# Graph attention on one core: transposes between projection chunks, denominators from three terms, batches written out

## The reference, cut to what matters

```python
h = jnp.maximum(_layernorm(x), 0.0)            # x: (8, 1024, 512)
q, k, v = heads(h @ Wq + bq), heads(h @ Wk + bk), heads(h @ Wv + bv)   # 16 heads of 32
scores = einsum('bhqd,bhkd->bhqk', q, k) / sqrt(32)
scores = where(adj[:, None] == 0, -inf, scores)
attn = softmax(scores, axis=-1)
out = einsum('bhqk,bhkd->bhqd', attn, v)       # heads side by side again: (8, 1024, 512)
return x + (out @ Wo + bo)
```

## Time and profile before

| | before |
|---|---|
| median of 3 runs (lowest to highest) | 2086.7 us (2085.78 to 2088.95) |
| the profiled execution: own time | 2085.51 us |
| the profiled execution: span of the trace | 2083.6 us |
| mean granted PE clock over the span | 0.989 |
| PE, DVE, ACT, POOL busy | 1932.5, 1557.3, 1478.1, 1302.1 us |
| chain that ended last | PE 76%, DVE 7%, issue 6%, DMA 5% |

### The profile page before, as it was taken

The page is one execution under the profiler, slowest core; times in us unless marked ns, Lnnn a source line. Parts: engine busy times, 40 slices in busy tenths (PEclk is TensorE's granted clock), DMA queues, the critical chain, the costliest instruction groups (busy, mean ns, idle before and its releaser), DMA issues.

```text
span 2083.6 us, 40441 instructions
## 1 busy us (share of the span) xinstructions
PE 1932.5 (93%) x14336; PEld 776.5 (37%) x14336; DVE 1557.3 (75%) x1587; ACT 1478.1 (71%) x1765; POOL 1302.1 (62%) x581
## 2 busy tenths in 40 slices
PE   3799899998999999999999999999899998999977
PEld 2334344343344333443334333334333343444312
DVE  5688777878768787687867877778767787767773
ACT  3577786677867788668876778767777677866672
POOL 0377567556666567656667557666557566676574
PEclk8999999999999999999999999999999999999999
DMA  5433244342444324343351434424234332442302
GB/s 177 122 87 96 82 112 132 88 107 64 120 112 124 83 76 132 86 122 86 92 142 56 115 93 117 119 74 119 81 109 122 88 106 66 117 122 64 74 1 81
DMA packets 103222, 206.61 MB, mean 99 GB/s; under 512 B 11616, under 2 KB 11744, under 8 KB 103008
## 3 DMA queue, kind: packets, MB, share of 16 engines
q1 hardware_dynamic: 103008, 203.80, 35.2%
HBM read 153.43 MB, written 50.33 MB: 98 GB/s over the span
## 4 chain that ended last, share of the span: by engine, by line
PE 76%; DVE 7%; issue 6%; DMA 5%; ACT 2%; POOL 1%; SPq 1%; DVEq 0%; ACTq 0%; POOLq 0%
PE ps L694 20%; PE ps L681 19%; PE ps L654 15%; PE ps L705 10%; PE ps L668 7%; PE ps L661 6%; DVE ring L905 4%; DMA k_stack<-k_parts 2%; DMA k_parts<-k_part 1%; SPq L513 1%; DMA edges<-adjT 1%; ACT hT_hi L776 1%; DVE k_part L918 1%; POOL acc L1079 1%; ACT ring L770 1%
## 5 line engine op out<-in xcount | busy, mean ns | idle before, releaser
L905 DVE TENSOR_TENSOR ring<-ps,mask 128x1024 f32<-128x1024 f32 x1024 | 1234.6, 1219 | 435.7 <-PE ps L681 399.9
L770 ACT ACTIVATE ring<-ring 128x1024 f32<-128x1024 f32 x1024 | 1069.7, 1051 | 382.9 <-DVE ring L905 374.6
L1079 POOL TENSOR_TENSOR acc<-ring 128x1024 f32<-128x1024 f32 x256 | 604.1, 2371 | 730.2 <-ACT ring L770 729.4
L681 PE MATMUL ps<-q_stack,k_stack 128*128 128x512 f16 x2048 | 610.4, 382 | 85.2 <-DVE ring L905 61.4
L1079 POOL TENSOR_TENSOR acc<-acc,ring 128x1024 f32<-128x1024 f32 x256 | 617.6, 2432 | 0.0
L694 PE MATMUL ps<-ring,v_sb 128*32 128x512 f32 x4096 | 509.1, 604 | 0.0
L681 PEld LDWEIGHTS ps<-q_stack,k_stack 128*128 128x128 f16 x2048 | 157.1, 98 | 481.8 <-DVE ring L905 246.4
L694 PEld LDWEIGHTS ps<-ring,v_sb 128*32 128x32 f32 x4096 | 100.9, 109 | 252.3 <-issue 218.1
L705 PE MATMUL ps<-acc,ones 128*32 128x512 f32 x1024 | 139.8, 597 | 2.7 <-issue 2.6
L705 PE MATMUL ps<-ring,ones 128*32 128x512 f32 x1024 | 137.3, 592 | 0.0
L661 PE MATMUL ps<-wv_hi,hT_hi 128*128 128x128 f16 x1024 | 103.1, 219 | 3.2 <-DVE k_part L918 3.2
(11 more groups left out here) (80 smaller groups left out, 1593.4 us busy)
## 6 DMA issues: line engine op xcount, KB each, us to landing
...
edges<-adjT SPq DMA_DIRECT2D x128, 256.0 KB, 2.9
q_stack<-q_parts SPq DMA_DIRECT2D x128, 256.0 KB, 4.9
k_stack<-k_parts SPq DMA_DIRECT2D x128, 256.0 KB, 5.0
...
```

Source lines behind the costliest of these rows:

```text
L681: i = nc.tensor.matmul(ps_s(j)[:, hh, :], stack["k"][:, up % 2, h, kt * P:(kt + 1) * P], stack["q"][:, up % 2, h, half * HALF:(half + 1) * ...
L770: nc.scalar.activation(tile, tile, ACT.Exp, scale=SCALE / UP / UP).then_inc(s["prob_ready"], 1)
L905: nc.vector.tensor_tensor(ring[:, slot_of(kt, pair), :].rearrange("p (a n) -> p a n", n=HALF), ps_s(j), mask[:, kt:kt + 1, half * HALF:(ha ...
L1079: nc.gpsimd.tensor_tensor(acc[:, group, pair, :], first_of, ring[:, slot_of(kt, pair), :], ALU.add).then_inc(s["sum_done"], 1)
```

## The change

Three things are changed together.

1. `BLOCKS` has four entries in place of five, the denominators have three terms in place of four (A, B and key tile 7): POOL adds key tiles 0 to 3 into A and 4 to 6 into B, ten additions a sweep in place of eight. The waits of POOL, DVE and PE on the sums follow.
2. The transposes have no slots of their own: they stand in `chunk_list` between the projection chunks of units 2 and 3, four in each, and the norms are in slot 29 of every unit. In unit 3 the second halves of q and k come behind all transposes. The slots in which x is normalised (by ACT) and loaded (by SP) follow.
3. The loops over batches 1 to 6 become Python loops on all engines: each batch is written out, with constants as semaphore targets.

```diff
-BLOCKS = {6: ("p0", "p1"), 10: ("p2", "p3", "dA"), 14: ("p4", "p5"), 16: ("p6", "dB", "d6"), 18: ("p7", "d7")}
-TERMS = "AB67"
+BLOCKS = {6: ("p0", "p1"), 10: ("p2", "p3"), 14: ("p4", "p5", "dA"), 18: ("p6", "dB", "p7", "d7")}
+TERMS = "AB7"
+SUMMED = {1: 0, 2: 2, 3: 4, 5: 6, 6: 8}
+SUMS = 10
+SUMMED_AT = {"A": 6, "B": 10}
...
-NORMALISE_AT = {(2, 5): 0, (2, 7): 1, (2, 9): 2, (2, 11): 3, (2, 23): 4, (2, 25): 5, (2, 27): 6, (2, 29): 7}
-T_AT = {(2, 19): 0, (2, 21): 1, (2, 23): 2, (2, 25): 3, (2, 27): 4, (2, 29): 5, (3, 1): 6, (3, 3): 7}
-SLOTS_OF = [SLOTS, SLOTS, [j for j in SLOTS if j <= 17], [j for j in SLOTS if j >= 5]]
-NORMS_AT = [29, 29, 18, 29]
+NORMALISE_AT = {(2, 5): 0, (2, 7): 1, (2, 9): 2, (2, 11): 3, (2, 21): 4, (2, 25): 5, (2, 29): 6, (3, 2): 7}
+NORMS_AT = 29
...
     if up == UNITS - 1:
-        return [] if last else ts + PROJ + [NORMS]
+        return [] if last else [q[0], ts[4], k[0], *ts[5:8], v[0], q[1], k[1], v[1], NORMS]
     if up == 2:
-        return PROJ + [NORMS] + ts
+        if last:
+            return [q[0], k[0], v[0], q[1], k[1], v[1], NORMS]
+        return [q[0], k[0], v[0], ts[0], q[1], ts[1], k[1], ts[2], v[1], ts[3], NORMS]
...
-            with pe.Fori(1, B - 1) as b:
+            for b in range(1, B - 1):
                 graph(b, False, False)
...
-                    pe.wait_ge(s["sum_done"], 8 * V + 4 * (TERMS.index(term) + 1))
+                    pe.wait_ge(s["sum_done"], SUMS * V + SUMMED_AT[term])
...
-                group, k = divmod(kt, 3)
+                group, n = kt // 4, SUMS * V + SUMMED[kt] + pair
                 pool.wait_ge(s["prob_ready"], U * TILES + j + 1)
...
-                        if j % SWEEP // PAIRS in (1, 2, 4, 5):
+                        if j % SWEEP // PAIRS in SUMMED:
                             sums(U, j, first and up == 0 and j < SWEEP)
```

More of the change, by code:

```diff
@@ L336, in chunk_plan @@
         return {}
-    plan = spread_out([c for c in chunks if c[0] != "t"], SLOTS_OF[up])
-    plan.update({at: [("t", t, 0, PIECES["t"])] for (u, at), t in T_AT.items() if u == up and ("t", t) in chunks})
-    return {**plan, NORMS_AT[up]: [(*NORMS, 0, PIECES["n"])]}
+    return {**spread_out(chunks, SLOTS), NORMS_AT: [(*NORMS, 0, PIECES["n"])]}
 def chunk_ends(up, first, last):
@@ L357, in count, with all_chunks, chunks_before, chunk_no @@
     return sum(c[0] in kinds for c in chunks)
[L360 to L374, removed]
-def two_before(b, up, first, chunk):
-    here = chunk_list(up, first, False)
-    i = here.index(chunk)
-    if i >= 2:
-        return b, up, first, here[i - 2]
-    if up:
-        return b, up - 1, first, chunk_list(up - 1, first, False)[i - 2]
-    if first:
-        return None
-    return b - 1, UNITS - 1, False, chunk_list(UNITS - 1, False, False)[i - 2]
+def all_chunks(b, up):
+    units = [(g, u) for g in range(b + 1) for u in range(UNITS) if (g, u) < (b, up)]
+    return [(g, u, c) for g, u in units for c in chunk_list(u, g == 0, g == B - 1)]
+def chunks_before(kinds, b, up):
+    return count(kinds, PRO_CHUNKS) + count(kinds, [c for _, _, c in all_chunks(b, up)])
+def chunk_no(kinds, b, up, chunk):
+    here = chunk_list(up, b == 0, b == B - 1)
+    return chunks_before(kinds, b, up) + count(kinds, here[:here.index(chunk)])
+def two_before(b, up, chunk):
+    here = chunk_list(up, b == 0, b == B - 1)
+    sequence = all_chunks(b, up) + [(b, up, c) for c in here[:here.index(chunk)]]
+    return sequence[-2] if len(sequence) >= 2 else None
 def fast_attention(nc, x, adjT, Wq, bq, Wk, bk, Wv, bv, Wo, bo, ident, headones, out, parts, flag):
@@ L438, in ps_s, with chunk_bank @@
             return ps[:, 2 * (j % 2):2 * (j % 2) + 2, :]
-        def chunk_bank(b, up, first, chunk):
-            n = chunk_no(ALL, 0 if first else 2, up, first, chunk) - len(PRO_CHUNKS)
+        def chunk_bank(b, up, chunk):
+            n = chunk_no(ALL, b, up, chunk) - len(PRO_CHUNKS)
             return ps[:, BANK_M + n % 2, :]
@@ L585, in graph @@
                             load_x(b + 1, (t + X_SLOTS) % QT)
-                        if (up, j - 1) in T_AT:
-                            t = T_AT[up, j - 1]
-                            sp.wait_ge(s["chunk_ready"], chunk_no(ALL, b, up, first, ("t", t)) + 1)
+                        for kind, t in ending_at(up, first, last, j - 1, "t"):
+                            sp.wait_ge(s["chunk_ready"], chunk_no(ALL, b, up, ("t", t)) + 1)
                             load_x(*((b + 1, t + X_SLOTS) if t + X_SLOTS < QT else (b, t + X_SLOTS - QT)))
@@ L599, in _ @@
             graph(0, True, False)
-            with sp.Fori(1, B - 1) as b:
+            for b in range(1, B - 1):
                 graph(b, False, False)
@@ L879, in _ @@
             graph(0, True, False)
-            with act.Fori(1, B - 1) as b:
+            for b in range(1, B - 1):
                 graph(b, False, False)
@@ L1040, in _ @@
             graph(0, True, False)
-            with dve.Fori(1, B - 1) as b:
+            for b in range(1, B - 1):
                 graph(b, False, False)
@@ L1104, in _ @@
             graph(0, True, False)
-            with pool.Fori(1, B - 1) as b:
+            for b in range(1, B - 1):
                 graph(b, False, False)
```

71 lines of the change are left out of this document (35 added, 36 removed).

## The result

| | before | after |
|---|---|---|
| median (lowest to highest) | 2087.8 us (2085.8 to 2091.1) | 2123.3 us (2118.9 to 2127.6) |
| the profiled execution: own time / span | 2085.5 / 2083.6 us | 2124.7 / 2122.9 us |
| ratio to before, 95% interval | | 1.0168 (1.0142 to 1.0195) |

The change makes the kernel 1.7% slower. The forecast was 2038.5 us, 85 us too low, and the measured time lies above the top of the range, 2074.

A forecast was written before the change was run, and what follows sets the result against it. The prediction took PE's instruction stream plus its waiting gaps as the bound. Unit terms gave 244.2 us a batch in place of 251.55, together -48 from 2085.5: 2037.5, or 2038.5 us as a median, range 1996 to 2074.

The forecast's parts named there:

- One term and block less: PE's stream, every sweep: one denominator term and one block fewer save 1.09 us, 8 sweeps, -8.7 us a batch.
- The loop: Starts of batches behind a loop return: straight code saves 4.2 us at each of five returns, -21 us.
- port term: SBUF port shared by DVE and POOL: o_low and additions block each other, 0.5 us in units 2 and 3 each.
- The new empty place: Unit starts: slots 31 and 0 have scores alone, +1.1 us at each of 31 starts, 4.5 a batch.
- Banks: Units 2 and 3: chunks behind short transposes wait for their bank's read-out, net +6.6 us a batch, from 0 to 9.
- Unit 2's gaps: PE's gaps in sparse slots go once pieces fill them: 6.5 us in unit 2, 2.5 in unit 3, -9 a batch.
- k's way through DRAM: End of unit 3: k1 ends in slot 24, so PE waits for k's load, +3.3 us.
- added waits come cheaper: Rival: bank and unit-start waits cost less than priced; with a third of them gone 2004 us; chance 0.20.
- the lock rules: Rival: the port lock makes each o_low wait some 1.9 us more, masks late in all 32 units, 2075 us; chance 0.11.
- POOL at dB: Rival: POOL's ten additions stretch to some 3.0 us and bound the kernel at dB in slot 2, 2140 us; chance 0.08.
- Straight code that stalls: Rival: straight code stalls at each instruction refill, so the 21 us stay, 2059.5 us; chance 0.08.
- The fifth: Rival: no net change, ACT's backlog and k's way cost double, +7 us a batch, about 2085 us; chance 0.05.

The follow-up runs named there:

- e2: e1 with the new blocks, three denominator terms and POOL additions, transposes as before the change: 2046.7 us, ratio 0.9804.
- e1: The kernel before with only its loop over batches written out, denominators and transposes as before: 2074.5 us, ratio 0.9938.
- e5: The changed kernel with p6 in a block of its own in slot 0, a fifth block, still three terms: 2105.7 us, ratio 1.0092.
- e7: e2 with p6 in a block of its own in slot 0, as in e5: 2027.1 us, ratio 0.9705.
- e10: e5 with a transpose piece costed 324 in place of 125, so more slots lie between the chunks around it: 2085.4 us, ratio 0.9985.
- e12: The changed kernel with 32 matmuls of unused result added in PE's wait for k_stack: 2111.7 us, ratio 1.0112.

## Why the prediction was wrong, step by step

**One term and block less**: right in sign and nearly in size. With the empty place it was to bring 34 us; e2 under e1 is 28. POOL's ten additions cost PE 2.9 us in all, and I took 0.

**The loop.** The return's 21 us were right as a price: 19.7 came back in units 0. e1 got only 13, because unit 2 lost 1.45 us a batch, nearly all of it with DVE and POOL in each other's way. I had no port term for straight code alone. In the kernel after, slot 8 of unit 2 has the 0.5 that was put for the port.

**The new empty place**: 1.1 forecast, 1.15 measured, and e5 and e7 confirm it by taking it away (17.7 and 19.6 us).

**Banks**: right, each wait within 0.4 us of its price.

**Unit 2's gaps**: -6.5 was the gain of filling empty slots, and here the first step fails. I let filled slots have no other waits. Unit 2 takes 60.4 us where the clock doesn't fall, and 57.7 were forecast. Two places have 2.3 us of waits for DVE and ACT that I had not put in, in slots 21 and 29. e10 shows that they belong in the main to the tight order: with room around the transposes slot 21's is gone, slot 29's is half as long, and unit 2 reaches 54.4.

**k's way through DRAM**: the step that failed. I carried 10.7 us from unit 1, lower half to first scores, over to unit 3 without asking what else was in SP's queue there. In batch 5 it is 1582.64 - 1567.23 = 15.4 us, 4.7 more. SP sent the store 1.1 us late and it took 7.0 us in place of 2.9, behind q's load; the load of k was 0.6 quicker. The rest of the term held: slots 25 to 30 last the 10.2 us of the forecast, and the lower half is done 2.7 us into slot 25 where 2.6 were put. That makes a wait of 7.9 us in place of 3.3, 4.6 a batch. A nearer row stood in the trace of the kernel before: its own k store in unit 3 took 3.6 to 3.8 us, not 2.9, with edges' loads around it and q's load long landed. The sentence that SP issues the same DMAs in about the same order was true of their order, not of their spacing: the transposes had pushed q1 and k1 together at the unit's end.

**Not in the sum at all: the granted clock.** Every term was taken from rows at 1.00, and the new waits brought the lower level back. Behind the k wait it costs 2 us a batch (e12), and 1.65 us in unit 2 of batches 4 and 5, where it falls (62.05 us against the 60.40 of batches 3 and 6, where it doesn't).

The misses by unit, means of batches 2 to 6 less forecast: unit 0 67.8 - 65.4 = 2.4, of which 2.0 the clock; unit 1 59.7 - 60.4 = -0.7; unit 2 61.5 - 57.7 = 3.8, of which 2.3 the small waits and 1.0 the clock; unit 3 66.9 - 60.7 = 6.2, of which 4.6 are k's. That is 11.7 a batch, 58 us in these five. Batches 0, 1 and 7 miss by 9.9, 7.9 and 12.5 us (236.5, 253.1 and, to the end, 286.4 us, against 226.6, 245.2 and 273.9 by the forecast). Together that is 88 us, about what the profiled execution misses by (2124.7 - 2037.5 = 87). Of unit 3's remaining 1.6 us, 0.6 are k0's and t7's waits above their prices (2.07 and 1.72), and in batches 2, 4 and 5 a stretch of 3.4 us at the lower clock lies behind k0's wait. The remaining 0.5 us of unit 2 I did not divide further.

**The rivals.** That added waits come cheaper was false: each is within 0.4 us of its price. That the lock rules was false in size: `o_low` takes 68.5 us in its 32 times where it took 58.1 before, 0.3 more each and not 1.9. The one on the slower side, POOL at dB, was false: 2.9 us of waits. Straight code that stalls was false in units 0. The fifth, no net change because ACT's backlog and k's way cost double, named k's way rightly, with 7 us a batch in all where it was 11.7, and a chance of 0.05. ACT's backlog was not it: q1's wait behind ACT's copy of v0 was 1.75 us where 2.1 were put. Of the signs of being wrong, one came in full, the period of 255.8 us, which is over 248, and one in small, the 2.9 us of PE's waits for POOL. The mechanisms of a slower kernel were in the prediction; I priced each from a place where it had room.
